# Linear attention's pipeline on one core: features behind the division, sums behind the output projection, projections last in the turn, ranks in columns of their own

## The reference

```python
feature = lambda a: elu(a) + 1.0
q, k, v = feature(x @ Wq.T), feature(x @ Wk.T), x @ Wv.T      # 16 heads of 8
kv, k_sum = einsum('bnhd,bnhm->bhdm', k, v), k.sum(axis=1)
numerator = einsum('bnhd,bhdm->bnhm', q, kv)
denominator = einsum('bnhd,bhd->bnh', q, k_sum)[..., None]
out = (numerator / (denominator + EPS)).reshape(b, n, d) @ Wo.T
logits = x2d @ router_w.T + router_b                           # of the next layer
vals, idx = top_k(logits, 2)
pos = cumsum(one_hot(idx)) - 1; kept = pos < capacity
```

## Time and profile before

| | us |
|---|---|
| median of 3 runs | 1482.45 |
| lowest and highest | 1482.42, 1483.17 |
| the profiled execution, first to last instruction | 1482.9 |
| linear attention, first sums to the last dispatch (from the timeline) | 1149.6 to 1304.9 |
| last expert layer, from its first turned tile | 1309.0 to the end |
| busy: PE, DVE, ACT, POOL | 1181.1, 831.8, 732.6, 726.9 |

### The profile page before, as it was taken

How to read it: one execution, slowest core, us unless ns; L and a number is a source line. 1 busy time by engine, 2 the same in 40 slices (tenths; PEclk the granted TensorE clock), 3 DMA queues, 4 the chain that set the end, 5 groups by cost and what they waited for, 6 DMA issues and landing times.

```text
span 1482.9 us, 23348 instructions
## 1 busy us (share of the span) xinstructions
PE 1181.1 (80%) x7329; PEld 784.2 (53%) x7329; DVE 831.8 (56%) x2723; ACT 732.6 (49%) x1494; POOL 726.9 (49%) x968
## 2 busy tenths in 40 slices
PE   3379997799999999999539998339998665469994
PEld 3268886222233233222239887328797554348894
DVE  7711454878899999887222566522127476512235
ACT  4234442467777767777324555214445456224441
POOL 3768654203323454534635477745554166535553
PEclk9999999799999999999869999669999788579997
DMA  9367977535435434331057886425576031135586
GB/s 288 122 166 227 263 213 236 148 100 158 134 103 159 132 81 139 116 96 30 27 153 230 240 244 205 143 75 184 159 228 203 4 125 33 35 109 173 171 264 201
DMA packets 164073, 226.83 MB, mean 153 GB/s; under 512 B 20656, under 2 KB 123440, under 8 KB 163952
## 3 DMA queue, kind: packets, MB, share of 16 engines
q1 hardware_dynamic: 119152, 174.05, 40.8%
q0 software_dynamic: 18304, 37.65, 7.5%
q10 hardware_dynamic: 26496, 13.64, 3.2%
HBM read 152.81 MB, written 72.20 MB: 152 GB/s over the span
## 4 chain that ended last, share of the span: by engine, by line
PE 53%; DVE 20%; DMA 10%; POOL 6%; issue 5%; SPq 3%; ACT 2%; ACTq 0%; POOLq 0%; DVEq 0%
PE PS L1329 16%; PE PS L1319 15%; DVE arena L2109 6%; PE PS L1451 5%; PE PS L1428 4%; POOL dispatched L703 2%; PE PS L1309 2%; DMA YC<-expert_out 2%; DMA arena<-experts 2%; PE PS L1436 2%; DVE BST L1704 2%; PE PS L1414 2%; DMA expert_out<-arena 2%; POOL dispatched L889 2%; DVE X L1714 1%
## 5 line engine op out<-in xcount | busy, mean ns | idle before, releaser
L729 POOL DMA_INDIRECT expert_out<-arena x316 | 304.1, 962 | 296.5 <-issue 191.3
L963 ACT ACTIVATE arena<-PS,arena 128x256 f32<-128x256 f32 (+1 forms) x568 | 267.6, 498 | 366.4 <-PE PS L1319 353.8
L1057 ACT ACTIVATE arena<-PS 128x512 f32<-128x512 f32 x512 | 286.5, 596 | 122.8 <-PE PS L1428 120.7
L2109 DVE TENSOR_REDUCE arena<-PS 128x2 f32<-128x1024 f32 x256 | 302.6, 1218 | 23.3 <-PE PS L1438 22.5
L1319 PE MATMUL PS<-arena 128*128 128x256 f32 (+1 forms) x1136 | 306.3, 413 | 8.5 <-DMA arena<-experts 7.2
L1329 PEld LDWEIGHTS PS<-arena 128*128 128x128 f32 x2528 | 302.7, 191 | 17.8 <-issue 3.3
L1329 PE MATMUL PS<-arena 128*128 128x128 f32 x2528 | 306.0, 275 | 2.4 <-DVE arena L1981 1.8
L1981 DVE TENSOR_TENSOR arena<-PS,arena 128x256 f32<-128x256 f32 (+1 forms) x142 | 64.5, 454 | 363.7 <-PE PS L1329 363.7
L1319 PEld LDWEIGHTS PS<-arena 128*128 128x128 f32 x1136 | 209.2, 194 | 57.8 <-DMA arena<-experts 10.2
L703 POOL DMA_INDIRECT dispatched<-arena x192 | 185.6, 966 | 82.3 <-issue 60.0
L1428 PE MATMUL PS<-arena 96*128 96x512 bf16 x512 | 170.3, 386 | 10.4 <-ACT arena L1057 4.2
(11 more groups left out here) (258 smaller groups left out, 1230.5 us busy)
## 6 DMA issues: line engine op xcount, KB each, us to landing
arena<-experts SPq DMA_DIRECT2D x142, 578.0 KB
qk_products<-arena SPq DMA_DIRECT2D x48, 384.0 KB, 4.4
arena<-qk_products SPq DMA_DIRECT2D x64, 288.0 KB
arena<-dispatched SPq DMA_DIRECT2D x110, 129.0 KB, 2.6
dispatched<-FILL SPq DMA_DIRECT2D x32, 322.5 KB, 2.7
YC<-expert_out ACTq DMA_DIRECT2D x40, 256.0 KB
arena<-qk_products SPq DMA_DIRECT2D x64, 128.0 KB, 5.0
arena<-dispatched SPq DMA_DIRECT2D x32, 193.5 KB, 3.0
```

The source lines that it names most:

```text
L729: pool.indirect_dma_start(YK, bass.IndirectOffsetOnAxis(ap=ID[:, s:s + 1], axis=0), YS[:, s, :], None).then_inc(s_yo[r], 16)
L963: act.activation(HT[:, tau % PAIR, q, 0:S * P], hidden_chunk(S, q), func, bias=WE[:, r, 2 * DFF + q:2 * DFF + q + 1]).then_inc(s_g, 1)
L1057: act.activation(PT[:, G % 2, j, k, :], bank(4 + k % 2), ACT.Exp, scale=float(1.0 / np.sqrt(HD))).then_inc(s_exp, 1)
L2109: dve.tensor_reduce(MX[:, G % 2, head:4:2, a], PS[:, 1024 * w:1024 * w + 1024].rearrange("p (a b) -> p a b", a=2), AX_X, ALU.max).then_inc ...
```

## The change

On TensorE the sums of batch 0 and the projections of batch 1 move ahead of the loop. In the loop a turn now begins with the numerators; the logits stand directly behind the turned route rows and ahead of `turn_out`; the next batch's sums stand behind this batch's output projection; and the projections of batch i + 2 stand behind its front, at the end of the turn. On ScalarE `features` is split in two, `negative_parts` and `exps`, with the route's scaling between them; the route's centring moves from the end of a turn to the start of the next; the front's centring moves ahead of `out_rows`, its scaling ahead of `second_rows`. On VectorE the features of batch i + 1 stand behind the division of batch i and ahead of the choice. The ranks go to columns 192 to 255 of bank 4, and the sums now wait until the logits of batch b - 2 have been read (`s_lgc`), the second batch's until the first one's sums have been masked. GpSimd's and SyncE's programs stay as they are. The line numbers behind the edits shift: by 1 on ScalarE, by 9 to 11 on TensorE and VectorE.

```diff
--- before.py
+++ after.py
@@ -63,6 +63,7 @@
 LATE = 16
 
 XCHUNKS = NG
+LRANK = 192
 ROUTER = E0 + GT * E0
 RING = 4
 XRING = 8
@@ -1147,7 +1148,7 @@
                         act.wait_ge(s_lk, b)
                     act.activation(XT[:, 0, :], bank(0), ACT.Copy).then_inc(s_l1c, 1)
 
-                def features(b):
+                def negative_parts(b):
                     u = b % 2
                     kv = PS[:, 1024:2048].rearrange("p (a b) -> p a b", a=GT)
                     act.wait_ge(s_lq, b + 1)
@@ -1159,6 +1160,9 @@
                         act.wait_ge(s_kv, b - 1)
                     act.activation(LV[:, u, :, 0:D], kv[:, :, D:2 * D], ACT.Copy).then_inc(s_lv, 1)
                     act.activation(LKM[:, u], kv[:, :, 0:D], ACT.Relu, scale=-1.0).then_inc(s_lmin, 1)
+
+                def exps(b):
+                    u = b % 2
                     act.wait_ge(s_lmin, 2 * b + 2)
                     act.activation(LQE[:, u], LQM[:, u], ACT.Exp, scale=-1.0).then_inc(s_lqe, 1)
                     act.activation(LKE[:, u], LKM[:, u], ACT.Exp, scale=-1.0).then_inc(s_lke, 1)
@@ -1185,25 +1189,30 @@
                        .then_inc(s_row, 1)
 
                 front_rows(0)
-                features(0)
+                negative_parts(0)
+                exps(0)
                 front_rows(1)
                 for i in range(NG + 1):
                     if batch(i - 1):
+                        batch_centre(i - 1)
+                    if batch(i + 1):
+                        negative_parts(i + 1)
+                    if batch(i - 1):
                         batch_scale(i - 1)
                     if batch(i + 1):
-                        features(i + 1)
+                        exps(i + 1)
                     if batch(i - 1):
                         batch_rows(i - 1)
+                    if batch(i + 2):
+                        front_centre(i + 2)
                     if batch(i):
                         out_rows(i)
+                    if batch(i + 2):
+                        front_scale(i + 2)
                     if batch(i - 1):
                         second_rows(i - 1)
                     if batch(i + 2):
-                        front_centre(i + 2)
-                        front_scale(i + 2)
                         front_rows(i + 2)
-                    if batch(i):
-                        batch_centre(i)
 
             for L, kind in enumerate(SUBLAYERS):
                 if kind in (FFN0, FFN1):
@@ -1606,8 +1615,10 @@
                 def sums(b):
                     pe.wait_ge(s_lkf, b + 1)
                     pe.wait_ge(s_lv, b + 1)
+                    if b == 1:
+                        pe.wait_ge(s_bd, 1)
                     if b >= 2:
-                        pe.wait_ge(s_pl, NG + b - 1)
+                        pe.wait_ge(s_lgc, NG * f + b - 1)
                     for j in range(GT):
                         mm = pe.matmul(bank(4, 0, D + 1), LKF[:, b % 2, j, :], LV[:, b % 2, j, :],
                                        start=(j == 0), stop=(j == GT - 1))
@@ -1657,32 +1668,32 @@
                     mm.then_inc(s_lg, 1)
 
                 def ranks(r):
-                    rank_tokens(bank(4, 0, GT * E1), r, E1, NG * f + r + 1)
+                    rank_tokens(bank(4, LRANK, LRANK + GT * E1), r, E1, NG * f + r + 1)
 
                 turn_front(0)
                 queries(0)
                 keys_values(0)
                 turn_front(1)
+                sums(0)
+                queries(1)
+                keys_values(1)
                 for i in range(NG + 1):
-                    if batch(i):
-                        sums(i)
-                    if batch(i + 1):
-                        queries(i + 1)
-                        keys_values(i + 1)
                     if batch(i):
                         numerators(i)
                     if batch(i - 1):
                         turn_rows(i - 1)
+                        logits(i - 1)
                     if batch(i):
                         turn_out(i)
+                        project(i)
+                    if batch(i + 1):
+                        sums(i + 1)
                     if batch(i - 1):
-                        logits(i - 1)
-                    if batch(i):
-                        project(i)
+                        ranks(i - 1)
                     if batch(i + 2):
                         turn_front(i + 2)
-                    if batch(i - 1):
-                        ranks(i - 1)
+                        queries(i + 2)
+                        keys_values(i + 2)
 
             for L, kind in enumerate(SUBLAYERS):
                 if kind in (FFN0, FFN1):
@@ -2270,9 +2281,9 @@
                     else:
                         chain(add_chosen(r, E, n))
 
+                features(0)
                 for i in range(NG + 1):
                     if batch(i):
-                        features(i)
                         by_head(i)
                     if batch(i + 2) and i + 2 >= FRONTS:
                         gather(f - 1, i + 2, 0)
@@ -2280,12 +2291,14 @@
                         lin_moments(i + 2, s_l1v)
                     if batch(i):
                         divide(i)
+                    if batch(i + 1):
+                        features(i + 1)
                     if batch(i - 1):
                         choose(i - 1)
                     if batch(i):
                         residual(i)
                     if batch(i - 1):
-                        place(i - 1, E, bank(4, 0, GT * E), NG * f + i)
+                        place(i - 1, E, bank(4, LRANK, LRANK + GT * E), NG * f + i)
 
             for L, kind in enumerate(SUBLAYERS):
                 if kind in (FFN0, FFN1):
```

## The result

| | us |
|---|---|
| changed kernel, median of 4 runs | 1464.89 |
| its lowest and highest | 1461.17, 1472.14 |
| kernel before beside it, median of 4 runs | 1482.43 |
| ratio, 95% interval | 0.989, 0.987 to 0.991 |
| the profiled execution, its span | 1466.09, 1464.3 |

The forecast was 1465.0, in a range from 1461.5 to 1473. The medians lie 17.5 us apart, the spans of the two profiled executions 18.6. Where did the 18.6 us come from? From here on "the stage" is the stretch from batch 0's route set to the end of the last dispatch, as GpSimd's timeline gives it. It took 1304.92 - 1163.82 = 141.1 us before and takes 1287.11 - 1162.34 = 124.8 now: 16.3 of the 18.6. The rest lies in stages whose order didn't change: the stage begins 1.5 us earlier, and what follows it is 0.8 shorter.

A forecast was written before the change was run, and what follows sets the result against it. A chain of waits across VectorE, TensorE and ScalarE, 17.22 us a batch, was taken to bound the linear attention stage. Earlier start 2.5 + waits gone 15.0 = 17.5 us; 1482.9 - 17.5 = 1465.4, as median 1465.0, range 1461.5 to 1473.

The forecast's parts named there:

- The bound becomes GpSimd, 14.8 to 15.1 us a batch: Linear attention stage: GpSimd's eight dispatches (10.5 us) and two sets (4.3) become the longest work per batch.
- One sign of being wrong: Linear attention stage: route sets over 16 us apart would show the prediction wrong; 15.0 to 15.3 expected for batches 2 to 5.
- Batch 1's set 2.5 us earlier: Start of GpSimd's unbroken run: batch 1's deviation set starts at 1177.2 in place of 1179.67.
- 15.0 of 15.5 us of waits gone: GpSimd's nine waits for VectorE's moments, 15.5 us in all, go except 0.5 left for the last batches.
- Cover: VectorE's moments arrive some 3 us before GpSimd asks for them, about 1 us behind the gathers.
- the loop that I took for the next bound: From a finished deviation set through scale, exponentials, copy, logits, choice, residual and moments: 9.4 us with hand-overs.
- Features, sums, own columns for the ranks, each at "no time": Features can't hold the choice; sums' wait on copied logits costs 0, at most 0.5 us a batch; rank columns no time.
- The tail: Sixteen dispatches behind batch 7's set, 20.1 us, keep their length and move with that set.
- Stretched dispatches: Rival, 0.13: 48 GpSimd dispatches beside denser VectorE work take 1067 in place of 958 ns, 5.2 us; 1470.2 us.
- Shrunken waits: Rival, 0.17: TensorE still drops to 1.2 GHz, half of GpSimd's 15.5 us of waits stays; about 1474.7 us.
- A slow loop: Rival, 0.05: TensorE never leaves 1.2 GHz, its own work becomes the loop, 18.1 us a batch; about 1488.5 us.

The follow-up runs named there:

- the four kernels with more or less work for GpSimd: Kernel before and changed kernel, each with 12 more GpSimd power operations (1480.78, 1478.71 us) or without the second choices' 32 of 64 dispatches (1477.19, 1454.27 us).
- the other chip: The changed kernel run again unaltered, on a chip where the kernel before takes 1572.95 us; 0.990 of the kernel before.
- the kernel with half the dispatches: Changed kernel without the second choices' dispatches in the linear attention stage (32 of 64 left out); 1454.27 us, 0.980 of the kernel before.
- split front: Changed kernel with the four refining operations of the front's set moved from GpSimd to VectorE; 1469.71 us, 0.990 of the kernel before.
- third kernel: The split front, plus route sets of batches 6 and 7 on VectorE and ScalarE's route scaling ahead of the negative parts; 1462.50 us, 0.986 of before.
- late features: Changed kernel with the next batch's features behind the placing, as before, and TensorE's sums behind the ranks; 1592.61 us, 1.013 of the kernel before.

## Why the prediction was right

- **The bound becomes GpSimd, 14.8 to 15.1 us a batch.** Right: 15.31 to 15.53 measured, and the four kernels with more or less work for GpSimd show it on both sides. Part of what is missing is longer instructions: in the trace the ten sets are busy 0.8 us longer in all and the dispatches 0.2. The rest is my average: a turn has two dispatches directly behind a set, of 1.06 us with a gap of 0.52, which over all 64 count for less; the eight of batch 5's turn come to 10.7 us and not 10.5. One sign of being wrong did appear, sets over 16 us apart, in batch 2 alone (16.76 us); the 1.80 us issue gap accounts for it, and the kernel before had it too.
- **Batch 1's set 2.5 us earlier.** From batch 0's set it came after 13.02 us in place of 15.85: 2.8 us. Right, and for the reason given: directly behind the projection TensorE is still at 2.4 GHz, the sums take 1.06, the queries 1.12, keys and values 1.89. (The 1.35 that I took for the sums at this clock was a row granted only 0.80.) From the projection's end at 1159.86 to the set are 15.5 us for the 15.9 worked out. Inside that path one piece is another than I named: the residual waits for batch 1's projection, 2.08 us at 1.2 GHz, and not for the choice.
- **15.0 of 15.5 us of waits gone.** 14.6 went; 1.0 came back as longer instructions, so 13.5 of the stage's 16.3.
- **Cover.** Right in size for most batches, wrong in its working. I had 3 us in turns with gathers and 1 us behind them. The moments of batches 3, 4 and 5 (these rows are their last operation) are ready 2.1, 3.3 and 2.2 us before GpSimd takes them at 1207.65, 1223.01 and 1238.32:

```profile
1205.42 0.18 DVE L2234 TENSOR_SCALAR LN<-LN 128x4 f32<-128x4 f32 x1
...
1219.61 0.15 DVE L2234 TENSOR_SCALAR LN<-LN 128x4 f32<-128x4 f32 x1
...
1235.98 0.17 DVE L2234 TENSOR_SCALAR LN<-LN 128x4 f32<-128x4 f32 x1
```

  Those of batch 2 come 0.4 us before, batch 6's 0.8, and for batch 7 there is no cover: GpSimd waited 0.87 us, and 1.85 on the other chip. But the loop that I took for the next bound is too short. From set to set my 9.4 us make 11.5 with the set's own 2.15, and the kernel with half the dispatches shows 13.67. I left out that the scale stands behind the copies of keys and values, that the residual waits for a projection which stands behind the logits and the turned output, and a clock of 1.2 GHz in part of it (that projection takes 2.07 us). So the next bound lies 1.7 us under GpSimd's 15.4, whatever the rows above show of slack.
- **Features, sums, own columns for the ranks, each at "no time".** As waits they cost nothing, as forecast: the sums never waited for the copied logits. But it was wrong to read the columns as a detail. Neither can be left out: without the features' place the time is 2.4% above the changed kernel, without the columns 1.3%, each with the order of sums and ranks that goes with it. ScalarE's new order is the part that could be left out.
- **The tail** keeps its length: 22.70 us from batch 7's set to the end, 22.67 before.
- **The total** of 1465.0 was near 1464.89 also by luck: the stage gave 16.3 where I had 17.5, and stages that did not change gave 2.3 us.

The rivals. Stretched dispatches: from batch 1's set to batch 5's VectorE is busy 0.80 of the time, 0.72 before, and the median dispatch is 959 ns against 958. Two took 1.21 and 1.22 us where the longest before was 1067 ns; on the other chip the longest was 1078. By the exclusive port lock of the Trainium skill ("SBUF — State Buffer", section "SBUF: two separate sides") a denser VectorE could hold GpSimd up more, where its operations run in a two-port mode; whether any here does, no run shows. The trace shows at most some 1 us of longer GpSimd instructions in the whole stage, most of it in the sets. Shrunken waits: TensorE does fall to 1.2 GHz within the turns of this kernel, but GpSimd's work hides it. As soon as GpSimd was relieved it showed, in the split front's alternating turns. A slow loop: a TensorE without idle time appeared in no run; even without the columns, at 0.68 granted, it is busy for 13.3 of 19.4 us from set to set.

On that clock: in the split front's long and short turn it is 0.75 and 0.81, in the third kernel's 1.00, with TensorE busy 12.56, 10.88 and 8.66 us for nearly the same instructions (61, 59 and 59). The Trainium skill ("TensorE: Matmul & The Clock Gate", section "HAM oscillation — how this bites in real kernels") tells how a wait in every step of a loop can leave each next step at the lower clock. The long turn is such a step, with queries of 2.07 us; the short one is not (1.12), so this explains half of the alternation at most. What tips it was not isolated here.

## What to carry to other kernels

When a change frees an engine that waits, ask for the longest of all loops behind it and count every in-order neighbour in each: slack in the trace is worth something only down to the next loop, and here that was 1.7 us where the rows show 2 to 3. Adding a known amount of work to the engine in doubt, in both kernels, tells in one run whether it is the bound. Sharing a buffer between steps of neighbouring batches can cost more than a reordering gains: here 1.3% against 1.0% on the same chip.

## What the hardware showed

- The kernel before took 1482 to 1484 us in three sets of runs and 1572.95 in the fourth, on another chip. The change's ratio was the same, 0.990, and so were the turns of linear attention. The time is lost in other stages, 86.8 of the changed kernel's 90.7 us of span ahead of batch 0's route set; the windows of the first 200 us, first of the changed kernel as in the result, then of the same kernel there, show TensorE busy for 102.75 us in place of 138.86 and the DMA engines' share at 0.55 in place of 0.70:

```profile
0.00:200.00 200.00, 138.86 (x862) 123.22 (x863) 96.83 (x547) 76.57 (x168) 126.25 (x125) 0.99 0.70 211
```

```profile
0.00:200.00 200.00, 102.75 (x621) 91.97 (x622) 75.34 (x463) 58.47 (x127) 108.83 (x107) 0.98 0.55 164
```

- The 59 TensorE rows of one turn were busy 8.66 us where 1.00 was granted (scale first, whole kernel) and 12.54 where 0.67 was (late features).
- One dispatch, the sixth, has an issue gap of 1.79 or 1.80 us in both kernels and in all others in which GpSimd makes the whole front's set, with half the dispatches too. In the three where it makes only the power, no dispatch of the stage has such a gap. What it is wasn't tried.
